# Attention stages of a four-layer transformer: the maxima's split, the groups' normalisation and the leading casts move to GpSimd, and a group's statistics to other entries

## The reference

```python
x = x + _L0_xattn_ref(_layernorm(x, axis=-1), ctx_1024, ctx_1024, mask_1_bf0, L0_xattn_Wq, L0_xattn_Wk, L0_xattn_Wv, L0_xattn_Wo)
...
def _layernorm(x, axis=-1, eps=1e-05):
    m = jnp.mean(x, axis=axis, keepdims=True)
    v = jnp.var(x, axis=axis, keepdims=True)
    return (x - m) / jnp.sqrt(v + eps)
...
q = (Q @ Wq.T).reshape(B, S, H, Dk).transpose(0, 2, 1, 3)
k = (K @ Wk.T).reshape(B, S, H, Dk).transpose(0, 2, 1, 3)
v = (V @ Wv.T).reshape(B, S, H, Dk).transpose(0, 2, 1, 3)
scores = jnp.einsum('bhqd,bhkd->bhqk', q, k) / jnp.sqrt(jnp.float32(Dk))
attn = jax.nn.softmax(scores, axis=-1)
ctx = jnp.einsum('bhqk,bhkd->bhqd', attn, v)
```

## Time and profile before

| | us |
|---|---|
| median of 3 runs (lowest to highest) | 1463.12 (1462.66 to 1466.3) |
| the profiled execution | 1462.91 |
| its span, first to last instruction | 1461.1 |
| DVE busy | 987.4 (68%) |
| POOL busy | 538.6 (37%) |
| the three attentions, from the first to the last add to x | 47.1 to 222.9, 565.6 to 776.5, 858.2 to 1032.1 |

### The profile page before, as it was taken

The page is one execution under the profiler, slowest core; times in us unless marked ns, Lnnn a source line. Parts: engine busy times, 40 slices in busy tenths (PEclk is TensorE's granted clock), DMA queues, the critical chain, the costliest instruction groups (busy, mean ns, idle before and its releaser), DMA issues. The chain is left out here.

```text
span 1461.1 us, 34924 instructions
## 1 busy us (share of the span) xinstructions
PE 1174.6 (80%) x11141; PEld 920.6 (63%) x11154; DVE 987.4 (68%) x2918; ACT 667.0 (46%) x1423; POOL 538.6 (37%) x590
## 2 busy tenths in 40 slices
PE   4799994349999957789987879999799856499991
PEld 2577773238899825566673456667477655399991
DVE  4689886554533248988984678888487777766552
ACT  2467771115555403445564546666233343144440
POOL 3223303674324166534411242431121125652564
PEclk9999995559999957889998989999799988599996
DMA  7887733012223267435532177564200042133542
GB/s 181 205 217 192 184 93 129 30 56 75 82 91 108 66 158 188 116 101 150 144 84 51 52 170 177 144 160 106 87 1 0 6 147 76 53 120 107 147 144 70
DMA packets 140294, 163.33 MB, mean 112 GB/s; under 512 B 15240, under 2 KB 120734, under 8 KB 133196
## 3 DMA queue, kind: packets, MB, share of 16 engines
q1 hardware_dynamic: 131980, 145.38, 37.0%
q0 software_dynamic: 8192, 16.46, 4.0%
HBM read 111.19 MB, written 50.92 MB: 111 GB/s over the span
## 5 line engine op out<-in xcount | busy, mean ns | idle before, releaser
L604 DVE TENSOR_REDUCE A_neg_max<-A_s_bank 128x4 f32<-128x512 f32 x384 | 254.0, 688 | 54.3 <-PE A_s_bank L747 43.9
L464 ACT ACTIVATE A_probsT<-A_st_bank 128x512 f32<-128x512 f32 x384 | 222.3, 602 | 50.1 <-PE A_st_bank L760 48.7
L747 PE MATMUL A_s_bank<-A_k_stack,A_q_stack 72*128 72x128 bf16 x1536 | 159.0, 230 | 42.5 <-DMA A_q_stack<-q_scratch 22.3
L760 PE MATMUL A_st_bank<-A_q_stack,A_k_stack 128*128 128x128 bf16 x1536 | 153.6, 225 | 7.2 <-DVE A_q_stack L620 6.4
L760 PEld LDWEIGHTS A_st_bank<-A_q_stack,A_k_stack 128*128 128x128 bf16 x1536 | 113.0, 104 | 53.5 <-issue 43.5
L747 PEld LDWEIGHTS A_s_bank<-A_k_stack,A_q_stack 72*128 72x128 bf16 x1536 | 107.2, 102 | 57.3 <-DVE A_neg_max L604 30.0
L772 PE MATMUL A_pv_bank<-A_probsT,A_v_pad 128*32 128x128 f32 x3072 | 127.5, 284 | 1.0 <-issue 1.0
L2065 ACT ACTIVATE E_h<-E_h_bank,w_L_b 128x256 f32<-128x256 f32 x184 | 76.8, 471 | 73.2 <-PE E_h_bank L2165 72.1
L2177 PE MATMUL E_y_bank<-E_w,E_h 128*128 x736 | 90.3, 276 | 2.2 <-ACT E_h L2065 0.9
L2165 PE MATMUL E_h_bank<-E_xT,E_w_u 128*128 128x256 f32 x368 | 89.5, 388 | 0.0
L772 PEld LDWEIGHTS A_pv_bank<-A_probsT,A_v_pad 128*32 128x32 f32 x3072 | 74.2, 111 | 24.2 <-issue 2.7
(11 more groups left out here) (369 smaller groups left out, 2639.7 us busy)
## 6 DMA issues: line engine op xcount, KB each, us to landing
A_q_stack<-q_scratch SPq DMA_DIRECT2D x48, 576.0 KB
A_k_stack<-k_scratch SPq DMA_DIRECT2D x32, 576.0 KB
q_scratch<-A_q_parts SPq DMA_DIRECT2D x48, 192.0 KB
A_k_stack<-k_scratch SPq DMA_DIRECT2D x48, 192.0 KB
E_xe<-slots_in SPq DMA_DIRECT2D x53, 128.0 KB, 2.1
slots_out<-E_ye SPq DMA_DIRECT2D x53, 128.0 KB
A_ctxT<-in_ctxT SPq DMA_DIRECT2D x24, 256.0 KB, 9.3
k_scratch<-A_k_parts SPq DMA_DIRECT2D x32, 192.0 KB
```

Of the source, the lines that this page charges most:

```text
L464: act.activation(probsT[n % 2][:, c * HQ:(c + 1) * HQ, :], st_bank[c % 2][:, :].rearrange("k (a q) -> k a q", a=HQ), ACT.Exp, scale=scale) ...
L604: dve.tensor_reduce(neg_max[:, c * HQ:(c + 1) * HQ], s_bank[c % 2][:, :].rearrange("q (a k) -> q a k", a=HQ), AX.X, ALU.max, negate=True). ...
L747: last = pe.matmul(s_bank[c % 2][:, a * S:(a + 1) * S], q_stack[slot][0:COMBO, h, at:at + S], k_stack[slot][0:COMBO, h, at:at + S], start= ...
L760: last = pe.matmul(dst, k_stack[slot][:, h, at:at + S], q_stack[slot][:, h, at:at + S], start=True, stop=spread)
```

## The change

It moves four things and changes two places of the schedule.

- `split_max` goes from VectorE to GpSimd, for all tiles from the third on in A0 and A2 and from the eleventh on in A1 (`POOL_FIRST`). The maxima have two buffers instead of one.
- `normalise` goes to GpSimd from the third group on (in A1 from the fifth).
- The first cast of keys and queries to bf16 in A0 and A2, which ScalarE made as its second reading of prep_bank, is made by whoever runs `split_rest` (GpSimd, and VectorE for the first group), from the float32 copy. In A1 it was there already.
- GpSimd's instructions are written in the order of the entries: in entry b the split of the maxima of tile b + 2, then by b mod 4 the bias (0), the keys' split (1), the queries' split (2), the normalisation of group g + 3 (3).
- Statistics of group g + 3 are taken at places 4 and 6 (entries 2 and 3 of a group). In A0 and A2 they were at places 0 and 2; in A1 those of group g + 2 were at place 0.

```diff
@@ -104,12 +104,9 @@
         K2 = Q2 = None
         PLACE = {V: 0, K1: 2, X: 3, Q1: 4}
     U = V + 1
-    if rope:
-        NORM_AHEAD = 2
-        STATISTICS, NORMALISE = {0: range(GB)}, {2: range(GB)}
-    else:
-        NORM_AHEAD = 3
-        STATISTICS, NORMALISE = {0: range(0, 2), 2: range(2, GB)}, {6: range(0, 2), 7: range(2, GB)}
+    NORM_AHEAD = 3
+    STATISTICS = {4: range(0, 2), 6: range(2, GB)}
+    POOL_FIRST = 2 * GB if late else 0
 
     def uses_at(place, g):
@@ -118,7 +115,7 @@
     QL, KL = (Q2, K2) if rope else (Q1, K1)
 
 
-    dve_steps = 2 * (GB * 2 + GB)
+    dve_steps = 2 * (GB + GB)
     CREDIT = 2
 
     ctx = ExitStack()
@@ -310,16 +307,13 @@
 
         def split_rest(eng, own, src, parts, rows, g, use, lead, done):
 
+            eng.wait_ge(prep_free, U * g + use + 1)
+            core.settle(eng)
             if rope:
-                eng.wait_ge(prep_free, U * g + use + 1)
-                core.settle(eng)
                 own.link(eng.tensor_tensor(src[:, :], src[:, :], rot_f[:, :], ALU.add))
                 core.settle(eng)
-                eng.tensor_copy(parts[:, 0, :], src[:, :]).then_inc(lead, 1)
-                eng.wait_ge(lead, g + 1)
-            else:
-                eng.wait_ge(lead, g + 1)
-                eng.wait_ge(prep_free, U * g + use + 1)
+            eng.tensor_copy(parts[:, 0, :], src[:, :]).then_inc(lead, 1)
+            eng.wait_ge(lead, g + 1)
             core.settle(eng)
             own.link(eng.tensor_tensor(split_r[0:rows, :], src[:, :], parts[:, 0, :], ALU.subtract))
             core.settle(eng)
@@ -328,6 +322,18 @@
             eng.tensor_tensor(parts[:, 2, :], split_r[0:rows, :], parts[:, 1, :], ALU.subtract).then_inc(done, 1)
             eng.wait_ge(done, g + 1)
             core.settle(eng)
+
+        def split_max(eng, own, b, n):
+
+            eng.wait_ge(max_done, 4 * (b + 1))
+            if not (isinstance(b, int) and b == 0):
+                eng.wait_ge(mt_ready, b)
+            core.settle(eng)
+            own.link(eng.tensor_copy(max_parts[:, hi:hi + NH], neg_max[n % 2][:, :]))
+            core.settle(eng)
+            eng.tensor_tensor(max_parts[:, lo:lo + NH], neg_max[n % 2][:, :], max_parts[:, hi:hi + NH], ALU.subtract)\
+                .then_inc(m_split, 1)
+            eng.wait_ge(m_split, b + 1)
 
         def values(eng, g, p):
 
@@ -379,6 +385,16 @@
                 own.link(pool.tensor_scalar(rstd[:, :], mv[:, :, 1], LN_EPS, None, ALU.add))
                 pool.tensor_tensor(rstd[:, :], rstd[:, :], core.minus_half[:, 0:GB], ALU.pow)\
                     .then_inc(rstd_done, 1)
+
+            def normalise(g):
+
+                inverse_deviation(g)
+                pool.wait_ge(rstd_done, g + 1)
+                pool.wait_ge(prep_ready, U * (g - 1) + X + 1)
+                for j in range(GB):
+                    last = pool.tensor_scalar(xn[:, j, :], core.x_tile(g * GB + j), mv[:, j, 0:1],
+                                              rstd[:, j:j + 1], ALU.subtract, ALU.mult)
+                last.then_inc(xn_done, 1)
 
             def add_bias(g):
@@ -420,26 +436,20 @@
                     split_rest(pool, own, k_f, k_parts, kd, g + 2, KL, k_lead, k_split)
                     late_rows(10 + 5 * g, min(12 + 5 * g, 16))
                     split_rest(pool, own, q_f, q_parts, D, g + 2, QL, q_lead, q_split)
-            for g in range(2):
-                add_bias(g)
-            if not rope:
-                inverse_deviation(2)
-                for g in range(2, NG):
-                    split_rest(pool, own, k_f, k_parts, kd, g, KL, k_lead, k_split)
-                    if exists(g + 1):
-                        inverse_deviation(g + 1)
-                    split_rest(pool, own, q_f, q_parts, D, g, QL, q_lead, q_split)
-                    add_bias(g)
-            else:
-                first = own.n
-                steps = 1 + 2 * 3
-                with pool.Fori(first_round, last_round) as it:
-                    for gg in range(2):
-                        own.start(first + ((it - first_round) * 2 + gg) * steps)
-                        inverse_deviation(it * 2 + gg + 2)
-                        split_rest(pool, own, k_f, k_parts, kd, it * 2 + gg + 2, KL, k_lead, k_split)
-                        split_rest(pool, own, q_f, q_parts, D, it * 2 + gg + 2, QL, q_lead, q_split)
-                        assert own.n == steps
+            add_bias(0)
+            normalise(4 if late else 2)
+            for b in range(POOL_FIRST, NB):
+                g = b // GB
+                if has_scores(b + 2):
+                    split_max(pool, own, b + 2, b)
+                if b % GB == 0 and exists(g + 1):
+                    add_bias(g + 1)
+                if b % GB == 1 and exists(g + 2):
+                    split_rest(pool, own, k_f, k_parts, kd, g + 2, KL, k_lead, k_split)
+                if b % GB == 2 and exists(g + 2):
+                    split_rest(pool, own, q_f, q_parts, D, g + 2, QL, q_lead, q_split)
+                if b % GB == 3 and exists(g + 3):
+                    normalise(g + 3)
 
         @block.scalar
         def _(act):
@@ -481,12 +491,11 @@
@@ -481,12 +491,11 @@
-                for to, done in ((dst[:, :], lead), (parts[:, 0, :], prep_free)):
-                    if shared_kv:
-                        ins = act.activation(to, prep_bank[0:rows, :], ACT.Identity, bias=bias)
-                    else:
-                        ins = act.copy(to, prep_bank[0:rows, :])
-                    ins.then_inc(done, 1)
+                if shared_kv:
+                    ins = act.activation(dst[:, :], prep_bank[0:rows, :], ACT.Identity, bias=bias)
+                else:
+                    ins = act.copy(dst[:, :], prep_bank[0:rows, :])
+                ins.then_inc(prep_free, 1)
 
             def take(use, g, p):
                 if use == X:
@@ -554,6 +563,8 @@
 
             def statistics(at, tiles=range(GB)):
 
+                if tiles[0] == 0 and not (isinstance(at, int) and at < 2):
+                    dve.wait_ge(xn_done, at)
                 for j in tiles:
                     own.did(dve.bn_stats(stats[:, j, :], core.x_tile(at * GB + j)))
                 own.wait()
@@ -599,20 +608,12 @@
                 elif rope and use in (Q1, Q2):
                     rotate(g, use, q_f, q_parts, q_split, qw_done, 2, q_lead)
 
-            def row_max(b, c):
+            def row_max(b, n, c):
+                if c == 0 and not (isinstance(b, int) and b < 2):
+                    dve.wait_ge(m_split, b - 1)
                 dve.wait_ge(s_ready, 4 * b + c + 1)
...
+                dve.tensor_reduce(neg_max[n % 2][:, c * HQ:(c + 1) * HQ], s_bank[c % 2][:, :].rearrange(
                     "q (a k) -> q a k", a=HQ), AX.X, ALU.max, negate=True).then_inc(max_done, 1)
-
-            def split_max(b):
-
-                dve.wait_ge(max_done, 4 * (b + 1))
-                if not (isinstance(b, int) and b == 0):
-                    dve.wait_ge(mt_ready, b)
-                own.link(dve.tensor_copy(max_parts[:, hi:hi + NH], neg_max[:, :]))
-                dve.tensor_tensor(max_parts[:, lo:lo + NH], neg_max[:, :], max_parts[:, hi:hi + NH], ALU.subtract)\
-                    .then_inc(m_split, 1)
-                dve.wait_ge(m_split, b + 1)
 
             def spread_max(b, n):
@@ -667,13 +668,12 @@
                         split_rest(dve, own, q_f, q_parts, D, g, QL, q_lead, q_split)
             for b in range(2):
                 for c in range(4):
-                    row_max(b, c)
-                split_max(b)
+                    row_max(b, b, c)
+                split_max(dve, own, b, b)
             if spread:
                 spread_max(0, 0)
-            if NORM_AHEAD == 3:
+            if not late:
                 statistics(2)
-                normalise(2, 2)
 
             def late_result(i):
@@ -691,28 +691,33 @@
                         at = 2 * (n % GB) + j
                         if begin and (n, at) == (GB, 0):
                             dve.wait_ge(begin.x_loaded[2], 16)
-                        if at in STATISTICS and exists(ahead):
+                        if late and isinstance(it, int) and it == 0:
+                            if at == 0:
+                                statistics(n // GB + 2)
+                            elif at == 2:
+                                normalise(n // GB + 2)
+                            elif (n, at) == (7, 6):
+                                statistics(4)
+                        elif at in STATISTICS and exists(ahead):
                             statistics(ahead, STATISTICS[at])
-                        if at in NORMALISE and exists(ahead):
-                            normalise(ahead, ahead, NORMALISE[at])
                         for use, g in uses_at(at, it * 2 + n // GB):
                             if exists(g):
                                 prep(use, g, (n // GB + (1 if use == V else 2)) % 2)
 
                     if has_scores(b + 2):
```

(12 more changed lines are left out.)

27 lines of the change are left out of this document (12 added, 15 removed).

## The result

The changed kernel takes 1475.82 us (median of 8 runs, 1470.88 to 1480.86) where the kernel before takes 1463.3 (8 runs): 1.009 times, interval 1.0072 to 1.0108. The forecast, 1452 us, was wrong in sign as well as in size. The profiled execution has a span of 1475.5 us against 1461.1.

A forecast was written before the change was run, and what follows sets the result against it. VectorE was taken to set the pace, TensorE close behind, with the queries' chain cutting off most of the gain; A0 -1.1, A2 -6.3, A1 -3.7 sum to -11.1 us, giving 1452 us, range 1439 to 1463.

The forecast's parts named there:

- the keys' split: GpSimd's split of keys: 4.1 us, in A1 6, there over just in time; 4.1 + 0.8 fits an entry of 5 us.
- a bound just above 20: Steady groups: without the chain TensorE would be next, busy 21.1 of 22.1 us including some waits; bound just above 20 us.
- The chain: Queries split by GpSimd, stored, loaded as a stack for later scores; parts done 10.4 us after first scores, 3.2 later than before.
- A pass is 21.7 us: A0 and A2 queries' way: 5.5 + 0.8 + 4.1 us, then 11.3 through memory; cuts off most of VectorE's gain.
- Its own load is hidden: GpSimd gets some 8 us more in a group, where 14 of 22 us are free.
- The contention term: VectorE's spread of the maxima beside GpSimd's work: up to 0.37 us longer in each of 13 passes, 4.8 us, time 1457.
- The third: Rival: GpSimd late with the maxima, TensorE stalled at their transpose; 1.3 us longer per pass, +17 us, 1469; chance 0.12.
- The first rival: The chain doesn't bind, so VectorE's 3.4 us a group come through down to TensorE: -26 us, 1437; chance 0.13.
- The second: Rival: A0 and A2 way through memory 12.3 us rather than 11.3; 10 passes lose 10 us, 1462; chance 0.13.
- The ratio of GpSimd to VectorE: Subtraction with a 128x512 bf16 result: 1.16 us on GpSimd, 0.69 on VectorE, ratio 1.7; moved work goes into free time.

The follow-up runs named there:

- E10: Kernel before, with maxima of all tiles but the first two not split and normalising cut to one column from group 2 on: 1452.15 us, 0.9937.
- E12: Changed kernel, but maxima on VectorE, normalising right behind the queries' split, and A0's and A2's statistics back at places 0 and 2: 1459.42 us, 0.9992.
- E2: Changed kernel, but VectorE splits the maxima of each group's third entry again: 1474.76 us, 1.0098 against the kernel before.
- E17: E5 plus two small GpSimd operations per entry on an idle tile, without waiting for the maxima: 1461.21 us, 0.9992 against the kernel before.
- E5: Changed kernel, but VectorE splits all maxima again; GpSimd keeps normalising and the casts: 1463.9 us, 1.0007 against the kernel before.
- E18: E5 plus a GpSimd wait for the last maxima in each entry, with no operation there: 1473.15 us, 1.0061 against the kernel before.
- E16: Changed kernel, but VectorE splits the maxima of entries 0, 2 and 3; GpSimd keeps those of the second entry: 1472.47 us, 1.0071 against the kernel before.
- E14: Changed kernel with GpSimd's normalising cut to one column: 1475.3 us, 1.0092 against the kernel before.
- E8: Changed kernel, but maxima and normalising on VectorE, casts on ScalarE; new statistics places and GpSimd's queue by entries stay: 1466.39 us, 1.0034 against the kernel before.
- E13: E5 plus, in each entry, GpSimd waiting for the maxima and making two split-sized operations on an idle tile: 1473.64 us, 1.0067 against the kernel before.
- E15: Changed kernel, but VectorE splits the maxima of each group's first entry: 1473.42 us, 1.0082 against the kernel before.
- E9: Changed kernel, but normalising on VectorE and casts on ScalarE, so of these GpSimd has only the maxima's split: 1467.03 us, 1.0029 against the kernel before.

## Why the prediction was wrong

Two steps of the working failed: the bound behind VectorE, which was taken to leave 2 us a group to win, and the keys' split, whose new wait was put at nothing. The chain's terms were too short as well.

**What bounds the kernel.** The working took VectorE as setting the pace and TensorE as next, with "a bound just above 20". This failed. TensorE's busy time per A0 group stays at 20.7 to 21.3 us in every kernel read here; E10 shows 21.4 us as what is left when the moved work costs nothing. With 22.09 before there was 0.7 us a group to win there, not 2. A0's sixth group, 20.86 us from add to x to add to x before, gives nothing: it takes 21.31 us in E10. Such a figure holds to about half a us: E12, which does all the work, has four groups of 21.2, 21.3, 20.4 and 20.8 us in A0 where E10 has 21.4, 21.2, 20.7 and 21.3.

**The chain.** Place and kind were right: a wait for A_q_stack once a group, parts done behind the last maxima. Its size was not. "A pass is 21.7 us" measured 23.13: maxima 5.89 for 5.5, their split 0.98 for 0.8, queries 4.28 for 4.1, memory 11.98 for 11.3. From group 3 to group 7 of A0 the four passes take 92.2 us (108.43 to 200.61) where the working had 86.0, 6.2 of the 8.3 us between forecast and measurement. But E2 shows that taking the chain away gives nothing back: the waits for the maxima grow to 3.4 us in two groups, and the groups stay at nearly the same length.

**What GpSimd takes over.** "Its own load is hidden" holds for the work (E17, E5); the wait that was put into its queue is not hidden. The text named who stands behind the maxima's split, but priced it for the queries alone. The keys' split, which began before the maxima and now waits for them, was costed at nothing in A0 and A2; E18 shows that GpSimd's waits for the maxima cost 0.6% by themselves, and E16 that the one ahead of the keys' split is enough for it. That they do so by moving both splits to where they hold VectorE is seen in single groups and argued for the rest. The contention term, +4.8 us at most for a spread of up to 1.06 us, was of the right kind and too small: the spread reached 1.68 in the changed kernel, and in E16 and E18 the maxima's split was held too.

**Edits costed at nothing.** Normalising at 918 ns cost nothing on the path (E14). The statistics' new places weren't given a cost: E8, which has them and no move, is 0.3% slower than before, though it also normalises at other places and writes GpSimd's queue by entries, so it does not show the places alone.

**The rivals.** The third had the sign, and its 1469 us was the nearest of all figures. Its mechanism, TensorE stalled by late maxima, is seen (2.0 us in two groups, the longest wait there and so the sign that the prediction named for it), but E13 has the loss without it, and E15 doesn't mend it: its figure is near by luck in part. The first rival's 1437 us lies below what leaving the work out gives. The second, all given back through 12.3 us of memory, had nearly the right size for that term: 11.98 to 12.14 us in the three passes of A0 that waited for the stack at 132.03, 155.16 and 178.30.

**GpSimd beside VectorE.** The ratio of GpSimd to VectorE, 1.7 by the rows read, was 2.7 for normalising, and did not decide. The Trainium skill ("SBUF — State Buffer", section "SBUF: two separate sides") says more than the page cited in the prediction: the pair of ports that the two engines share is locked for a whole instruction by whoever starts first, where VectorE's operation has two inputs in SBUF or runs in a mode that uses two ports. The traces agree for E16's subtraction, which has two inputs in SBUF: normally 0.18 us, it ended with GpSimd's cast that had started 0.02 us before it, at 136.21 and 136.18.

**What stays open.** How much of the changed kernel's own 12.5 us is the chain, the waits for maxima and the held spread was not separated; the kernels that remove one (E2, E15, E13) show another at about the same length. The +4.7 us outside the attentions was not traced; it lies within the range of the profiles there, 900.2 to 905.2 us. The maxima alone on GpSimd (E9) bring such waits too and, net of what VectorE gives up, cost nothing that is seen against E8; why they cost only with the casts or normalising beside them is open.

## What to carry to other kernels

A wait placed in an in-order queue is paid by all that stands behind it, not by the work that it guards: price every later item of that queue by when it could start before and when it can start now. Before moving work off the busiest engine, read the second busiest's own work in the same stretch, since that is what is left to win; leaving the work out in a trial gives that number. Parts that are free alone can cost together, so test them in combination.

## What the runs showed of the hardware

- A normalisation of 128x128 with two per-row scalars took 896 to 918 ns on GpSimd on average and 344 on VectorE, 2.6 to 2.7 times; two-input subtractions with a 128x512 bf16 result stood at 1.16 against 0.69 us, 1.7 times.
- A small operation of VectorE (0.18 us for 128x16) that meets a GpSimd cast of 0.61 us ended when the cast ended (E16, E18). Where GpSimd and VectorE were released by the same maxima they met more often: VectorE's cast has a mean of 464 ns over A2 in E18, with 16 of 30 above 0.4 us, and 270 in E17, which has no such wait, with 6 of 29.
- Maxima (L615), reads of PSUM with small results, took 0.680 to 0.694 us in the changed kernel, beside GpSimd or not, and VectorE's statistics stayed below 0.30. Copies, casts and subtractions in SBUF were held: a spread of 0.69 us took up to 1.68.
